# Layer 3's local attention: sums of probabilities by TensorE with a block of ones, division where outputs leave PSUM

## The reference, cut to what matters

```python
def local_attention(q, k, v):          # b=4, h=8 heads, n=512, d=64, WINDOW=64
    ...
    sim = jnp.einsum('bhwid,bhwjd->bhwij', bq, bk)    # 64 queries x 128 keys a window
    mask = (i < j) | (i > j + WINDOW) | (j == -1)
    sim = jnp.where(mask, -jnp.finfo(sim.dtype).max, sim)
    attn = jax.nn.softmax(sim, axis=-1)
    out = jnp.einsum('bhwij,bhwjd->bhwid', attn, bv)
    return out.reshape(b, h, n, d)

x = x + 0.5 * _L3_ffn_ref(_layernorm(x, axis=-1), ...)   # two layers, each with local_attention
x = x + _L3_attn_ref(_layernorm(x, axis=-1), ...)
x = x + 0.5 * _L3_ffn_ref(_layernorm(x, axis=-1), ...)
```

## Time and profile before

| | |
|---|---|
| median of three runs | 3219.22 us (3215.2 to 3230.39) |
| profiled execution | 3222.13 us |
| its span | 3220.3 us |
| mean granted TensorE clock, of 1 | 0.894 |
| instructions | 64240 |

### The profile page before, as it was taken

One profiled execution on the slowest core, in us unless ns is written; L12 is line 12 of the kernel. 1 busy time (PEld: TensorE's weight loads), 2 busy tenths in 40 slices (PEclk: granted clock), 3 DMA queues, 4 the chain that ended last, 5 costly groups with the idle time before them and its releaser, 6 DMA issues.

```text
span 3220.3 us, 64240 instructions
## 1 busy us (share of the span) xinstructions
PE 2716.4 (84%) x24502; PEld 1722.2 (53%) x24561; DVE 2240.2 (70%) x5340; ACT 1693.2 (53%) x4134; POOL 848.8 (26%) x875
## 2 busy tenths in 40 slices
PE   5857788898886789998777888899998888999996
PEld 2545455544444444467755777556563332465664
DVE  4656567788876668864466545887887677788783
ACT  2235443565622365542357434676765666776772
POOL 1010001122111222112233124555541112555550
PEclk8767777899977799998899999999998888999997
DMA  2524410000000000036510366100100000101010
GB/s 104 219 38 66 65 51 1 1 1 1 1 1 1 1 1 1 1 125 247 188 54 2 122 229 202 42 21 21 26 16 3 1 1 1 24 16 26 16 33 10
DMA packets 136844, 159.38 MB, mean 49 GB/s; under 512 B 84949, under 2 KB 111829, under 8 KB 135002
## 3 DMA queue, kind: packets, MB, share of 16 engines
q1 hardware_dynamic: 134010, 150.09, 15.7%
q0 software_dynamic: 2048, 4.20, 0.4%
q10 hardware_dynamic: 480, 0.98, 0.1%
HBM read 106.53 MB, written 30.61 MB: 43 GB/s over the span
## 4 chain that ended last, share of the span: by engine, by line
PE 49%; DVE 23%; ACT 8%; issue 5%; POOL 4%; DMA 3%; SPq 2%; POOLq 0%; DVEq 0%; ACTq 0%
DVE nm L1181 5%; PE ps L1915 4%; PE ps L1140 4%; PE ps L529 3%; PE ps L2117 3%; PE ps L1117 3%; PE ps L1081 3%; PE ps L2283 3%; ACT hand L494 2%; PE ps L387 2%; DMA hand<-in_experts 2%; PE ps L602 2%; PE ps L266 2%; PE ps L2420 2%; PE ps L1900 1%
## 5 line engine op out<-in xcount | busy, mean ns | idle before, releaser
L1181 DVE TENSOR_REDUCE nm<-ps 128x2 f32<-128x256 f32 (+2 forms) x704 | 428.5, 644 | 104.3 <-PE ps L1081 50.2
L1230 ACT ACTIVATE core<-ps 128x512 f32<-128x512 f32 x672 | 360.8, 588 | 100.4 <-PE ps L1122 61.4
L2189 POOL TENSOR_TENSOR pre<-pre,sin 128x512 f32<-128x512 f32 x128 | 236.9, 1871 | 251.7 <-ACT pre L2160 211.0
L328 POOL TENSOR_TENSOR rstd<-ve,weights 128x4 f32<-128x4 f32 x80 | 81.0, 1013 | 843.1 <-DVE ve L305 839.2
L1081 PE MATMUL ps<-hand 128*128 128x128 bf16 (+4 forms) x993 | 239.4, 319 | 46.9 <-DVE nm L1181 42.1
L494 ACT COPY hand<-ps 64x512 bf16<-64x512 bf16 x320 | 185.5, 580 | 152.0 <-PE ps L529 95.3
L1117 PE MATMUL ps<-hand 128*128 128x128 bf16 (+4 forms) x996 | 213.4, 305 | 9.6 <-ACT hand L494 5.4
L1915 PE MATMUL ps<-hand 128*128 128x128 f32 x1408 | 197.4, 300 | 25.5 <-DMA hand<-in_experts 25.4
L2194 POOL TENSOR_TENSOR ss<-ss,weights 128x16 f32<-128x16 f32 x64 | 199.2, 3112 | 72.9 <-DVE ss L2209 71.1
L2323 ACT ACTIVATE core<-ps,nm 128x128 f32<-128x128 f32 x512 | 182.1, 376 | 64.8 <-DVE nm L2340 64.3
L1915 PEld LDWEIGHTS ps<-hand 128*128 128x128 f32 x1408 | 188.1, 215 | 35.3 <-DMA hand<-in_experts 29.3
(11 more groups left out here) (339 smaller groups left out, 6663.9 us busy)
## 6 DMA issues: line engine op xcount, KB each, us to landing
hand<-in_experts SPq DMA_DIRECT2D x88, 836.0 KB, 8.0
shear<-post SPq DMA_DIRECT2D x64, 256.0 KB
core<-shear SPq DMA_DIRECT2D x256, 32.0 KB, 1.9
hand<-hand SPq DMA_DIRECT2D x16, 512.0 KB, 4.4
hand<-hand SPq DMA_DIRECT2D x16, 384.0 KB, 5.6
pre<-sorted_in SPq DMA_DIRECT2D x8, 704.0 KB, 4.9
sorted_out<-core SPq DMA_DIRECT2D x88, 64.0 KB
core<-in_stream SPq DMA_DIRECT2D x2, 2048.0 KB, 8.4
```

The costliest lines, as they stand in the source:

```text
L1181: nc.vector.tensor_reduce(nm_of(unit), src, AX.X, ALU.max, negate=True).then_inc(negmax, 1)
L1230: nc.scalar.activation(prob8[:, i % PROBS, 0:w], m.ps[:, RING[at % NR], 0:w], ACT.Exp).then_inc(ring_out, 1)
L2189: ins = nc.gpsimd.tensor_tensor(o[:, :, :, z:z + hl], x[:, :, :, y0:y0 + hl], sn[:, t, :, z:z + hl].unsqueeze(2).to_broadcast([P, 2, LH, h ...
```

## The change

The exponentials no longer accumulate sums, and the probabilities are not scaled. Behind the eight output matmuls of a unit TensorE multiplies a block of ones (64 columns of the 128x128 constant "ones") by the turned probabilities: the two matmuls, one for each head, write each query's sum into 256 columns of bank 4, the same in all 64 output partitions of that head. A unit's outputs now take columns 0 to 255 of bank 4, its sums columns 256 to 511. VectorE then takes the reciprocal of the 128x256 sums into SBUF (m.inv, in the core buffer) and writes outputs times reciprocals to otok. This happens for each of the eight units instead of one copy for every two; the next unit's output matmuls wait for it. The buffers sums and rsum are gone.

```diff
@@ -2241,8 +2241,8 @@
     NP3, NT3 = 3, 3
     TURN, WEIGH = 2, 3
     S, PT, O = (0, 1), (2, 3), 4
-    scores, negmax, exps, inverted, scaled, turned, pT_ready, av, o_out = (note(n) for n in (
-        "scores", "negmax", "exps", "inverted", "scaled", "turned", "pT_ready", "av", "o_out"))
+    scores, negmax, exps, turned, pT_ready, av, inverted, o_out = (note(n) for n in (
+        "scores", "negmax", "exps", "turned", "pT_ready", "av", "inverted", "o_out"))
     left, ready = before.left.seen_by("l3_layer"), before.lane
     prob = m.core[:, 0:NP3 * L].rearrange("p (s n) -> p s n", s=NP3)
     pT = m.core[:, NP3 * L:(NP3 + NT3) * L].rearrange("p (s n) -> p s n", s=NT3)
@@ -2285,7 +2285,7 @@
                 ins.then_inc(scores, 1)
             if TURN <= i < U + TURN:
                 u = i - TURN
-                pe.wait_ge(scaled, u + 1)
+                pe.wait_ge(exps, 4 * (u + 1))
                 if u == 0:
                     left(pe, "turn banks")
                 if u >= 2:
@@ -2301,13 +2301,17 @@
                 if u == 0:
                     before.pre(pe)
                     before.core(pe)
-                if half == 0 and c >= 1:
-                    pe.wait_ge(o_out, c)
+                if u >= 1:
+                    pe.wait_ge(o_out, u)
                 for r in range(4):
                     n = 4 * half + r
                     for e in range(2):
-                        ins = nc.tensor.matmul(m.ps[64 * e:64 * e + 64, O, n * WIN:(n + 1) * WIN], value(n, c, e),
-                                               pT[:, u % NT3, r * P + 64 * e:r * P + 64 * e + 64], start=True, stop=True)
+                        nc.tensor.matmul(m.ps[64 * e:64 * e + 64, O, r * WIN:(r + 1) * WIN], value(n, c, e),
+                                         pT[:, u % NT3, r * P + 64 * e:r * P + 64 * e + 64], start=True, stop=True)
+                for e in range(2):
+                    both = pT[:, u % NT3, :].rearrange("p (r e q) -> p r e q", e=2, q=WIN)
+                    ins = nc.tensor.matmul(m.ps[64 * e:64 * e + 64, O, 4 * WIN:8 * WIN], m.weight["ones"][:, 0:64],
+                                           both[:, :, e, :], start=True, stop=True)
                 ins.then_inc(av, 1)
 
     def scalar(act):
@@ -2321,8 +2325,7 @@
                     act.wait_ge(turned, i - NP3 + 1)
                 for r in range(4):
                     nc.scalar.activation(prob[:, i % NP3, r * P:(r + 1) * P], bank(m, S[i % 2])[:, r * P:(r + 1) * P],
-                                         ACT.Exp, bias=m.nm[:, 4 * i + r:4 * i + r + 1],
-                                         accum_out=m.sums[:, 4 * i + r:4 * i + r + 1]).then_inc(exps, 1)
+                                         ACT.Exp, bias=m.nm[:, 4 * i + r:4 * i + r + 1]).then_inc(exps, 1)
             if i >= TURN:
                 u = i - TURN
                 act.wait_ge(turned, u + 1)
@@ -2339,32 +2342,25 @@
                 dve.wait_ge(scores, i + 1)
                 nc.vector.tensor_reduce(m.nm[:, 4 * i:4 * i + 4], blocks(bank(m, S[i % 2])), AX.X, ALU.max,
                                         negate=True).then_inc(negmax, 1)
-            if 1 <= i <= U:
-                u = i - 1
-                dve.wait_ge(exps, 4 * i)
-                nc.vector.reciprocal(m.rsum[:, 4 * u:4 * u + 4], m.sums[:, 4 * u:4 * u + 4]).then_inc(inverted, 1)
-                dve.wait_ge(inverted, i)
-                p = blocks(prob[:, u % NP3, :])
-                nc.vector.tensor_tensor(p, p, m.rsum[:, 4 * u:4 * u + 4].unsqueeze(2).to_broadcast([P, 4, P]),
-                                        ALU.mult).then_inc(scaled, 1)
             if i >= WEIGH:
                 u = i - WEIGH
                 c, half = units[u]
-                if half == 1:
-                    dve.wait_ge(av, u + 1)
-                    if c == 0:
-                        before.read(dve)
-                    nc.vector.tensor_copy(a.otok[:, c, :], bank(m, O)).then_inc(o_out, 1)
+                dve.wait_ge(av, u + 1)
+                if u == 0:
+                    before.read(dve)
+                nc.vector.reciprocal(m.inv, m.ps[:, O, 4 * WIN:8 * WIN]).then_inc(inverted, 1)
+                dve.wait_ge(inverted, u + 1)
+                nc.vector.tensor_tensor(a.otok[:, c, half * 4 * WIN:(half + 1) * 4 * WIN], m.ps[:, O, 0:4 * WIN],
+                                        m.inv, ALU.mult).then_inc(o_out, 1)
 
     def done(eng):
-        eng.wait_ge(o_out, 4)
+        eng.wait_ge(o_out, U)
...
-    {"tensor": "c1a2c3b1a1b1a1b3a1b2a1b2c1b1c1b1c1a1c1b1a1b1c1a1b2c1b2a1b1c1a1b1c1b2",
+    {"tensor": "c1a1c3b1a2b2a1b2a1b1a1c1b1a1b1c1b1a1c1b2c1b1a1c1b2c1b2c1a1b1c1b2a1b2",
...
```

More of the change, by code:

```diff
@@ L2710 @@
      "gpsimd": "d1b6c1b6",
+     "sync": "c1b1"},
+    {"tensor": "b1a2b2c4b1a1b2a1b2a1b3c1b1c1a1c1b2c1a1c1b1a1c1b1c1a1b1a1c1b2a1b2",
+     "vector": "b1a2b2c1b1a1c2b1c1a1c2b2c1a1b2a1b1a1b1c1a1c1b2a1c1b2a1b1c1b1c1a1",
+     "scalar": "b3a1b1a2b2a1b4c1a1c1b2c1a1b1c1a1c1b1a1b2a2b5",
+     "gpsimd": "b4c1b2d1b6",
+     "sync": "c1b1"},
+    {"tensor": "c1a1c2b1c1b1a1b1a1b2a1c1a1c1a1c1a1c1a1b1a1b1c1b1c1b1a1b1c1b1a1b1c1b1",
+     "vector": "b3a1b1c2a1c1a1c4b1a1b3a1b3a1b2a1b2a1b1c1a1c1b1a1c1b1a1c1b1c1",
+     "scalar": "a1b3a1b1a1b1a1c1a1c1a1b3c1a1c1a1b1c1b1a2b2",
+     "gpsimd": "b1c1b5d1"},
@@ new lines @@
+    {"tensor": ("a2c1a2c1a1c1a2c1a16b1a1b1a3b1a2b1a3c1a1b1a3c1a4c1a4c1a3c1a4c1a5b1a3b1a1c1b1a3b1a4b1a1c1a1b1a3b1a2b1a"
+         "14"),
+     "vector": ("a2b1a3b1a1b1a14b1c1a1c2a4c1a2c2a2c1a4b1a2b1a2b1a2b1a2b1a1b1a1b1a1b1a1b1a3c1a1b1a4b1a4c1b1a5b1c1a2c1b"
+         "1c1b1"),
+     "scalar": "a1b1a1b1a3b1a2b1a4c1b1a4c1a4c1a3c1a2c1a3b1a2b1a2b1a3b1a5b1a7b1a4b1a16",
+     "gpsimd": "b2a1c1a1b3d1b1a2"},
+    {"tensor": "a6c1a2b1a4b1a1c1a2b1a4c1a1b1a3b1a2c1a8c1a18c1a5b1a4b1a4b1a2b1a2b1a4b1a5b1a3b1a8",
+     "vector": "b4a11c1a3c1a7c1a8c1b1a3b2a1b1a4b1a4b1a3b1a4b1a1b1a1b1a3b1a6b1a5c1b3",
+     "scalar": "b4a6b1a6c1a13b2a3b1a6b1a8b1a4b1a7b1a13",
+     "gpsimd": "b2d1b1a3b3a1"},
@@ new lines @@
+    {"tensor": "a2b1a4b1a4b1a2c1a3b1a2c1a3b1a27c1a9b1a4b1a4b1a2b1a1c1a1b1c1a1b1a3b1a3c1a5b1a8",
+     "vector": "b4a13c1a9b2a7b1a3b1a1b1a2c1b1a4b1a6b1a3b1a2b1a3b1a4c1a4b1a3b1c1b1c1b1",
+     "scalar": "b5a20b1a7b2a8b1a7b1a4b1a3c1a1b1a16",
+     "gpsimd": "b2a2b2a1b1d1b1a1"},
+    {"tensor": ("a4b1a2c1a3b1a5b1a6b1a3b1a2c1a7b1a2b1a1b1c1a1b1a1b1a3b1a4b1a2b1a1c1a2b1a3b1a4c1a4b1a2b1a2b1a4c1a4b1a3"
+         "b1a6b1a7"),
+     "vector": "b4a7b1a6c1a7b1a7b1a4b1a1b1c1a1b1a2b1a4b1a4b1a1c1a4c1a1b1a2b1a6b1a3b1a4b2c1b2",
+     "scalar": "b4a8b1a2b1a2b1a1b1a1b1a1b1a4b1a3b1a3b1a2b1a7b1a4b1a2b1a2c1a3b1a6b1a2b1a5b1a8",
+     "gpsimd": "b1a1b3a1b4a1b4a1b1d1"},
@@ new lines @@
+    {"tensor": "b1a2b2c1a1b1c1b1a1b2a1b2c1b1a1b2a1b1c1b1a1b2c1b2a1b1a1c1a1b2",
+     "vector": "b5a2c1b1a1b1c1b1a1b2a1b2c1a1b1a1b2c1b1a1b3a1b1a1b1c1a1",
+     "scalar": "b1a1b2a2b2a1b3a1b2a1b2a1b4a1b2a1c1a1b3",
+     "gpsimd": "b13d1"},
+    {"tensor": "c1a1c1a1c1b1c1a1b4a1b1a1b1a1b2c1b1c1a1b1a1c1b1a1b2c1b1c1b1c1a1b2c1a1b1c1b2",
+     "vector": "b3a1b1a1c1b1a1c1b2c2a1c1b1c1a1b1c1a1b2a1b1a1b3a1b1c1b1c1b1a1b1c1a1b2c1",
+     "scalar": "a1b1a1b2a1b2a1b1a1b3c1a1b1a1c1b1a1c1b1a1b2c2b3a1b4",
+     "gpsimd": "b3d1b1c1b9",
+     "sync": "c1b1"},
@@ new lines @@
+    {"tensor": "c1a1c3b1a2b2a1b2a1b2a1c1a1c1b2c1b2c1b2a1b1c1b2c1a1b1c1b2a1c1a1b2",
+     "vector": "b3a1b1c2a1b1a1c3a1b1c1b1a1c1b1a1b3a1b4a1b1c1b1c1a1b2c1a1b2c1a1",
+     "scalar": "a1b1a2b2a1b2a1b1a1c1b1c1b2a1c1b2c1b2c1b1a1b3a1b1a1b3",
+     "gpsimd": "b1d1b1c1b11",
+     "sync": "c1b1"},
+    {"tensor": "c1b1c1a1b2c2a1b2a1b2a1b2a2b2a1b1c1a1c1b2c1b1a1c1b1c1a1b1c1b2c1a1c1b2",
+     "vector": "b1a1b1c1a1c2b1a1b1c1b1a1c2a1b1a1b1c1a1b2a1b3a1b2c1b1c1a1c1b2a1c1",
+     "scalar": "b3a2b2a1b2a2b2a1b2a1c1b1c1b1a1c1a1b2c1b1c1b1a1b4",
+     "gpsimd": "b5c1b1d1b6",
+     "sync": "c1b1"},
@@ new lines @@
+    {"tensor": "c1b1a2c1b2a1c2b2a1b1a1b1a1c1b2c1b1c1b1c1b1a1c1b2c1b2c1a1c1b1a1b2a1b2a1",
+     "vector": "b1a3b2c2b1c1a1c3a1c1b3a1b3a1c1b1c1b1c1b1a1b3c1a1b1a2",
+     "scalar": "b1a1b2a2b2a1b1a1b1c1b2c1b1c1a1b1c1b1c1b2a1b2a1b1a1b1a1b3",
+     "gpsimd": "b3c1b2d1b7",
+     "sync": "c1b1"},
+    {"tensor": "b1a1c1b2c2a1c1b2a1b2a1b2a1b2c1a1c1a1b1c1a1b1c1b1a1b1c1b1c1b1a1c1b2c1b2a1",
+     "vector": "b1a1b2a1c1b1c1a1c1b1c1a1c1b1c1a1c1b1a1b1a1b1a1b3a1c1b2c1b1c1b2a1c2a1",
+     "scalar": "b3a1b1a1b1a1b2a1b2a1c1b1a1c1b1a1c1b1a1b1c1b1c1b2a1b3a1b2",
+     "gpsimd": "b3c1d1b9",
@@ L2716 @@
      "sync": "c1b1c1"},
[L2717 to L2718 removed]
+    {"tensor": "a2b2a1b2a3b2a1b1a1b2a1b3a2",
+     "vector": "a3b3a1b1a1b3a3b3a1b2a2",
      "scalar": "a5b1a1b1a1b1a1b2a2",
@@ L2836, in macaron @@
             work.append(w)
-        m.nm, m.sums, m.rsum = sb("nm", NT * H), sb("sums", NT * H), sb("rsum", NT * H)
+        m.nm = sb("nm", NT * H)
         m.aggv = sb("aggv", 2)
+        m.inv = m.core[:, 3072:3328]
         m.ss, m.beta = sb("ss", 2, NT * 2 * H), sb("beta", NT, H)
```

116 lines of the change are left out of this document (29 added, 87 removed).

## The result

Device time rose from 3217.21 us (median of 4 runs, 3212.1 to 3230.39) to 3340.11 us (3337.41 to 3349.4): the ratio is 1.0394, 95% interval 1.0355 to 1.0432, about +125 us. The forecast was 3324 us within 3268 to 3388 us. The profiled execution took 3337.58 us with a span of 3335.8 us, 115.5 us over the span before.

A forecast was written before the change was run, and what follows sets the result against it. TensorE was taken to bound layer 3's core slots, VectorE close behind. TensorE's added work (+86 us) plus 16 us for unmatched pieces gave +102 us on 3222.1 us, so 3324 us; forecast 3295 to 3370 us, wider range 3268 to 3388 us.

The forecast's parts named there:

- What bounds the kernel: Layer 3's core slots, two stretches of 828 us: TensorE sets the pace at 92.1% busy, VectorE follows at 81.0%.
- The main term of the sum: Core-slot stretches: TensorE's work grows from 763 to 842 us and lasts 914 us at 92.1% busy, +86 us.
- rival with a cheap reciprocal: Core slots: reciprocal takes only 0.42 us, TensorE still gains 79 us; +59 us, 3281 us; chance 0.10, shared with nearly full overlap.
- the ring: Bank 4: next unit's output matmuls wait for the division; 3.8 us against TensorE's 4.1 us, 16 us for unmatched pieces.
- VectorE, +142 us forecast: Core units: 162.3 us removed, 305 us added by 128 reciprocals of 1.96 us and multiplications of 0.42 us.
- TensorE, +79 us forecast: Core units: two f32 matmuls of ones at 0.62 us a unit, ratio 0.73 for partial overlap; bounds 54 to 109 us.
- ScalarE and the moved steps: Core slots: 109.6 us of accumulator reads go, counted as nothing; new orders, also one slot ahead, −5 to +5 us.
- Idle time: TensorE in the core stretches: 65 us idle before; afterwards the same busy share over 914 us, plus 16 us for unmatched pieces.
- The signs named: Profile after: reciprocal near 1.96 us, VectorE over 85% in layer-3 slots, slots of 52 and 56 us some 6 us longer.
- the worse ring: Core slots: waits between TensorE and VectorE cost 5 us a slot; +166 us, 3388 us; both stretches under 88% TensorE; chance 0.17.
- The other side: Core stretches: bf16-priced ones, 40 us, and a shorter chain to the transposes closing TensorE's holes; −20 us, 3202 us; chance 0.08.

The follow-up runs named there:

- Experiment 2: Changed kernel without the matmuls of ones; the reciprocal reads the outputs' own 256 columns: 3324.76 us, ratio 1.0351.
- the square: Changed kernel with and without the matmuls of ones, each with the long reciprocal or a plain copy: ratios 1.0394, 1.0351, 1.0115, 1.0032.
- experiment 7: Kernel before plus the matmuls of ones in each unit, written where the outputs then overwrite them; old orders: 3236.49 us, ratio 1.0059.
- experiment 1: Changed kernel with a plain copy of the 128x256 sums in place of their reciprocal: 3245.76 us, ratio 1.0115.
- experiment 4: Changed kernel without the matmuls of ones and with a plain copy in place of the reciprocal: 3214.58 us, ratio 1.0032.
- 7 to 10: Kernel before, old orders, with: matmuls of ones added; a 128x120 reciprocal added; scaling removed; scaling on GpSimd. Ratios 1.0059, 1.0177, 0.9970, 1.0651.
- experiment 6: Kernel before with only the changed kernel's table of orders, all work as before: 3278.39 us, ratio 1.0182.
- Experiment 3: Changed kernel with the reciprocal moved behind the multiplication, reading a constant table, so bank 4 is held for less time: 3310.77 us, ratio 1.0327.
- 8: Kernel before plus a 128x120 reciprocal from a constant table in each unit, no new wait for TensorE: 3274.89 us, ratio 1.0177.

## Why the prediction was right

The time lay inside the stated range, and the direction and the place of the loss were right. The sum behind it weighed the two engines wrongly, and that it came so near is in good part luck.

- *What bounds the kernel.* All the loss is in the core slots. The main term of the sum, TensorE's 842 us at an unchanged busy share of 92.1%, gave +86 us, and VectorE's added work was checked only for whether it fits. Experiment 2 takes all of TensorE's added work away and keeps 109 of the 120 us; the ones cost 11 to 14 us in the square and 26 us by themselves (experiment 7, at a busy share of 95%). The long reciprocal, to which the forecast and its rival with a cheap reciprocal leave 102 − 59 = 43 us, costs 96 to 99 us in the core slots. So the share of 92.1% was no ceiling, and the cost of VectorE's added work, which makes TensorE wait, was left out of the sum but for the 16 us of the ring.
- *VectorE, +142 us forecast.* 128 x (1.749 + 0.424) − 162.3 = +116 us. The reciprocal was put at 1.96 us and took 1.75, inside its bounds of 1.51 and 2.25. From 128 elements (950 ns) to 256 (1749 ns) it gains 6.2 ns an element. The prediction says that two pairs of the small rows agree on the slope of 7.1 ns. They don't: between 1 and 4 elements the rows give 4 ns, from either of these to 16 elements 6.5 to 8.3 ns.
- *TensorE, +79 us forecast.* 128 x 0.43 = 55 us by the starts; its busy time grew by 46 to 48 us where the clock stayed at 1.00 (experiments 1 and 7). The ratio 0.73, taken from matmuls of 64 columns, does not hold for 256 columns: the pairs overlap in full. The Trainium skill's "TensorEngine Tiling (Array Packing)", "Key Properties", says that different tiles can load weights and multiply in parallel; by estimate, with the trace's 0.83 ns a column and instruction, that is 0.43 us for the pair, and the trace agrees.
- *ScalarE and the moved steps.* Nothing was counted for ScalarE; experiment 4 gives no sign of a gain. The orders were put at nothing, −5 to +5 us. The part ahead of the core slots took 5.7 us less, but with the old orders (7 to 10) it took 3.6 to 12.9 us less as well, so this need not be an effect of the orders; and experiment 6 shows that the table's fit can be worth 59 us. That step wasn't argued well enough.
- *The ring.* It was said to close just inside TensorE's own work of a period, 3.8 against 4.1 us, by a shortest period of 3.4 us (the rows give 3.46). That is not the shortest. In the kernel before, two units in a row have their output matmuls 2.69 us apart:

```profile
2419.56 0.69 PE L2309 MATMUL ps<-core,hand 128*64 128x64 f32 x16 [0.55 <-ACT core L2333]
2422.25 0.69 PE L2309 MATMUL ps<-core,hand 128*64 128x64 f32 x16 [0.18 <-ACT core L2333]
```

  After, the period without projections shown above is 3.52 us, from 3019.31 to 3022.83, and TensorE stood for 0.47 us of it: the ring binds there.
- *Idle time.* This term was mis-sized. The same share at 914 us plus 16 us for the ring made some 23 us more idle time; measured are 49 us. Experiment 3 gives the ring at most 22 to 29 us; the rest comes with the load (8), also at the post stream's matmuls.
- *The clock.* This term was missing. TensorE's added busy time is 71.6 us. With the same instructions and the clock at 1.00 (experiment 1) it is 45.7 us; the other 26 us go with the lower clock.
- *The signs named.* VectorE at over 85% in these stretches did not come, it is at 83%. TensorE's share, 88.1% and 88.0%, lies at the border of what was named as the sign of the worse ring (under 88%), and +125 us lies between the forecast's +102 and that rival's +166 us. The slots last 7.5 us longer on average, where 6 was said.

The forecast's +102 us were 79 us of TensorE's work and 23 us of idle time. The core slots have 46 us of work, 49 us of idle time and 26 us of clock, 121 us together: a price that was too high stood against an idle term that was too low and a clock term that was missing. VectorE's price, 26 us too high, did not enter the sum. Of the rivals, the cheap reciprocal was run as experiment 1: forecast +59 us, measured +37 us, since the ones fill waits. The other side's shorter chain to the transposes, with neither the ones nor the long reciprocal, was experiment 4: it reaches the time of before and no less.

## What to carry to other kernels

Price a reciprocal by its elements a partition, not as an elementwise operation: 4 sums a partition took 0.17 us, the same division spread over 256 columns 1.75 us, ten times as much. With two engines near full, test each added load alone before trusting the busy shares: here 55 us on TensorE cost 19 us, 114 us on VectorE 57 us, and removing 97 us from VectorE brought 10 us. Read the added cost in the changed stage, between the same marks of each trace: the rest of the kernel differed by 10 us and more between executions here, as much as some of the effects in question. An order written for one set of durations should be made anew, and judged apart, when a duration changes.
